# Turned tiles of a masked-softmax graph layer: half of them sent through DMA as f16 parts instead of through TensorE

## What is computed

```python
Wh = x @ W.T
sim = Wh @ Wh.T / (norms * norms.T + 1e-8)
alpha = softmax(where((adj > 0) | eye(N), sim, -inf), axis=1)
x1 = layernorm(x + alpha @ Wh)
mask = (adj > 0);  deg = sum(mask, axis=1)
agg = mask @ x1 / maximum(deg, 1.0)
comb = concat([x1 @ W_self + b_self, agg @ W_nb + b_nb]) @ W_comb + b_comb
out = layernorm(x1 + relu(comb))
```

## Time and profile before

| | us |
|---|---|
| Median of 3 runs | 889.4 (888.64 to 890.17) |
| The profiled execution | 888.87 |
| Its span | 887.1 |
| PE busy | 871.4 (98%) |
| DVE busy | 578.8 (65%) |
| ACT busy | 390.9 (44%) |
| POOL busy | 66.1 (7%) |

### The profile page before, as it was taken

One profiled execution on the slowest core, in us unless ns is written; L12 is line 12 of the kernel. 1 busy time (PEld: TensorE's weight loads), 2 busy tenths in 40 slices (PEclk: granted clock), 3 DMA queues, 4 the chain that ended last, 5 costly groups with the idle time before them and its releaser, 6 DMA issues.

```text
span 887.1 us, 20117 instructions
## 1 busy us (share of the span) xinstructions
PE 871.4 (98%) x7039; PEld 705.1 (79%) x7039; DVE 578.8 (65%) x1252; ACT 390.9 (44%) x661; POOL 66.1 (7%) x177
## 2 busy tenths in 40 slices
PE   8989999999999999999999999999999999999997
PEld 7767777777777777777787777777888888888886
DVE  3777877878666787668767877889716333333333
ACT  4867656655656565556565656564310000000000
POOL 3400000000000000000000000011101000000000
PEclk9999999999999999999999999999999999999999
DMA  8977675555554745576549459575753303311300
GB/s 223 292 175 184 186 209 154 158 170 154 149 169 131 215 139 168 151 178 189 163 141 240 136 171 316 157 202 114 203 113 126 113 19 113 114 66 67 114 18 19
DMA packets 165204, 135.72 MB, mean 153 GB/s; under 512 B 79121, under 2 KB 142882, under 8 KB 164098
## 3 DMA queue, kind: packets, MB, share of 16 engines
q1 hardware_dynamic: 164930, 134.26, 53.3%
q0 software_dynamic: 192, 0.41, 0.2%
HBM read 95.83 MB, written 28.85 MB: 141 GB/s over the span
## 4 chain that ended last, share of the span: by engine, by line
issue 81%; PE 9%; POOL 5%; DVE 2%; ACT 1%; POOLq 1%; DMA 0%; DVEq 0%; SPq 0%; ACTq 0%
PE ps L1142 3%; POOL rstd L571 3%; POOL var_eps L569 1%; PE ps L1230 1%; PE ps L1232 1%; PE ps L1231 1%; PE ps L1170 1%; PE ps L1172 1%; PE ps L1171 1%; PE ps L1224 1%; ACT mask L639 0%; DMA feat<-xT 0%; ACT prob_hi L634 0%; DVE feat L747 0%; DVE work L890 0%
## 5 line engine op out<-in xcount | busy, mean ns | idle before, releaser
L1230 PE MATMUL ps<-feat,prob_hi 128*128 128x257 f16 (+1 forms) x1024 | 279.8, 273 | 1.1 <-DVE prob_lo L897 1.1
L1232 PE MATMUL ps<-feat,prob_lo 128*128 128x257 f16 (+1 forms) x1024 | 279.5, 273 | 0.0
L1231 PE MATMUL ps<-feat,prob_hi 128*128 128x256 f16 (+1 forms) x1024 | 278.9, 272 | 0.0
L897 DVE SCALAR_TENSOR_TENSOR prob_lo<-work,prob_hi 128x512 f16<-128x512 f32 x256 | 176.0, 687 | 83.4 <-ACT prob_hi L634 80.7
L1373 PE MATMUL ps<-big,mgroup 128*128 128x257 f16 x992 | 219.2, 273 | 0.0
L1374 PE MATMUL ps<-big,mgroup 128*128 128x256 f16 x992 | 219.2, 273 | 0.0
L634 ACT ACTIVATE prob_hi<-work 128x512 f16<-128x512 f32 x256 | 154.4, 625 | 86.4 <-DVE work L890 42.8
L627 ACT ACTIVATE work<-ps 128x512 f32<-128x512 f32 (+2 forms) x144 | 79.2, 556 | 134.8 <-PE ps L1172 116.6
L639 ACT ACTIVATE mask<-work 128x1024 fp8e4<-128x1024 f32 x128 | 133.6, 1043 | 0.0
L1231 PEld LDWEIGHTS ps<-feat,prob_hi 128*128 128x128 f16 x1024 | 100.3, 98 | 25.3
L1230 PEld LDWEIGHTS ps<-feat,prob_hi 128*128 128x128 f16 x1024 | 100.0, 98 | 25.1 <-issue 1.3
(11 more groups left out here) (130 smaller groups left out, 780.9 us busy)
## 6 DMA issues: line engine op xcount, KB each, us to landing
adj_sb<-adjT SPq DMA_DIRECT2D x128, 512.0 KB, 3.8
mask_spill<-mask SPq DMA_DIRECT2D x128, 128.0 KB, 2.7
mgroup<-mask_spill SPq DMA_DIRECT2D x8, 2048.0 KB, 8.0
xres<-x SPq DMA_DIRECT2D x8, 512.0 KB, 5.1
x1h_dram<-big SPq DMA_DIRECT2D x16, 256.0 KB, 5.2
out<-rows SPq DMA_DIRECT2D x32, 128.0 KB, 1.7
feat<-xT SPq DMA_DIRECT2D x7, 512.0 KB, 6.7
unit_dram<-feat SPq DMA_DIRECT2D x7, 512.0 KB, 4.4
```

Of the source, the lines that this page charges most:

```text
L897: dve.scalar_tensor_tensor(out=prob_lo[:, s, :], in0=prob[:, s, :], scalar=PROB_SCALE, in1=prob_hi[:, s, :], op0=ALU.mult, op1=ALU.subtrac ...
L1230: pe.matmul(acc(D + 1), prob_hi[:, s, cols], feat_hi_of(g)[:, r, 0:D + 1], start=start, stop=False)
L1231: pe.matmul(acc(D), prob_hi[:, s, cols], feat_lo_of(g)[:, r, :], start=False, stop=False)
L1232: return pe.matmul(acc(D + 1), prob_lo[:, s, cols], feat_hi_of(g)[:, r, 0:D + 1], start=False, stop=stop)
```

## The change

In rows 1 to 6 (`far(a)`) a pair's eight tiles come in another order and two of its turned tiles by another way:

- Direct tiles 0 and 1: ScalarE writes the high f16 part of the unmasked exponential to `far_parts` (`high`), VectorE the low one (`low`). Both are then masked by f16 products: `keep` turns two tiles of int32 adjacency into an f16 0/1 mask (`kept`, in the place of a `prob` slot pair), and `masked_parts` multiplies it by both parts straight into `prob_hi` and `prob_lo`. ScalarE copies `kept` to `mask` (`unit_kept`).
- Direct tiles 2 and 3: as before.
- Tiles 4 and 5, the turned ones of `expo` 2 and 3: four transposes by TensorE each (`block_scores`), masked from PSUM (`mask_blocks`). A tile is now one block of 128 targets against four source blocks, added up within one tile (`attend_block`) and copied by one sum (`block_copied`).
- Tiles 6 and 7, the turned ones of `expo` 0 and 1: SP stores `far_parts` (512 KB) to `far_dram` and brings each part back by a transposing DMA (256 KB each) into `far_turned`; a second `keep` and `masked_parts` mask them. TensorE does nothing for them ahead of the attend.

SP's order in a pair: `store_far` of the next pair stands ahead of the fourth adjacency load, `turn_far` behind the last mask store; both wait. The loops of rows 1 to 6 are written out on every engine. `far_parts` lies in the place of `rows`, half of `far_turned` in that of `w0T_sb`; `damp` is halved. Semaphore counts follow.

```diff
+        def far_turned(h):
+            if h:
+                return far_turned_lo[:, :, :]
+            return w0T_sb[:, :, :].bitcast(F16).rearrange("p k n -> p (k n)").rearrange("p (s i) -> p s i", s=GB)
+        def kept(slot):
+            return prob[:, slot, :].bitcast(F16)
+        def halved(ap):
+            return ap.rearrange("p (s i) -> p s i", s=GB)
...
+            def load_next(a, b, m, slot):
+                if not far(a):
+                    load_unit(a, b, m, slot)
+                elif m < 2:
+                    load_direct(a, b, m, slot)
+                else:
+                    load_turned(a, b, 3 - m, slot)
...
+            def store_far(a, b):
+                k = far_before(a) + b - a - 1
+                sync.wait_ge(far_lo_ready, 2 * (k + 1))
+                sync.dma_start(far_dram.rearrange("h r p i -> p h r i"), far_parts).then_inc(far_stored, 16)
+            def turn_far(a, b):
+                k = far_before(a) + b - a - 1
+                if k == 0:
+                    sync.wait_ge(mixw_ready, 2)
+                sync.wait_ge(far_stored, 16 * (k + 1))
+                sync.wait_ge(prob_lo_ready, tiles_before(a)[0] + GB + (b - a - 1) * STEP_TILES)
+                for h in range(2):
+                    sync.dma_start_transpose(far_turned(h), far_dram[h].rearrange("r p i -> (r p) i")).then_inc(far_loaded, 16)
+            def pair_far(a, b):
+                t0 = tiles_before(a)[0] + GB + (b - a - 1) * STEP_TILES
+                u0 = tiles_before(a)[2] + 2 + (b - a - 1) * 4
+                for m in range(4):
+                    slot = (u0 + m) % 4
+                    if m == 3 and b < G - 1:
+                        store_far(a, b + 1)
+                    sync.wait_ge(prob_ready, t0 + 2 * m + 2)
+                    if b < G - 1:
+                        load_next(a, b + 1, m, slot)
+                    elif m < 2:
+                        load_direct(a + 1, a + 1, m, slot)
+                    elif a + 2 < G:
+                        load_next(a + 1, a + 2, m - 2, slot)
+                    sync.wait_ge(mask_ready, u0 + m + 1)
+                    if m < 2:
+                        store_direct(a, b, m, slot)
+                    else:
+                        store_turned(a, b, 3 - m, slot)
+                if b < G - 1:
+                    turn_far(a, b + 1)
...
+            def unit_kept(u, s, count):
+                act.wait_ge(kept_ready, count)
+                wait(act, mask_stored[u % 4], 16 * (u // 4))
+                act.activation(mask[:, u % 4, :], kept(s), ACT.Copy, saturate=False).then_inc(mask_ready, 1)
...
+            def pair_far(a, b):
+                n = b - a - 1
+                t0, f0, u0 = (first + more for first, more in zip(tiles_before(a), (GB + n * STEP_TILES, GB + n * GB, 2 + n * 4)))
+                c0 = scores_before(a) + GB + n * 6
+                k = far_before(a) + n
+                if n == 0:
+                    act.wait_ge(mirror_done, (a + 1) * (GB - 1))
+                def high(r):
+                    act.wait_ge(exp_ready, f0 + r + 1)
+                    if k == 0:
+                        act.wait_ge(mixw_ready, 2)
+                    wait(act, far_stored, 16 * k)
+                    act.activation(far_parts[:, 0, r, :], expo[:, r, :], ACT.Copy, scale=PROB_SCALE).then_inc(far_hi_ready, 1)
+                for r in range(2):
+                    exponentials(t0 + r, c0 + r, f0 + r, r, GB)
+                    high(r)
+                unit_kept(u0, 0, 2 * k + 1)
+                for r in range(2, GB):
+                    exponentials(t0 + r, c0 + r, f0 + r, r, GB)
+                    heads(t0 + r, r)
+                unit_mask((u0 + 1) % 4, 2, 16 * ((u0 + 1) // 4))
+                heads(t0 + 4, 0)
+                heads(t0 + 5, 1)
+                unit_blocks(u0 + 2, 0)
+                unit_kept(u0 + 3, 2, 2 * k + 2)
...
+            def block_copied(b, block, t):
+                dve.wait_ge(attn_done, t + 1)
+                to = partial_of(b)[:, block, :]
+                dve.tensor_tensor(to, to, turned_ps(block % 2, D + 1), ALU.add).then_inc(turned_copied, 1)
+            def keep(u, s, parts):
+                dve.wait_ge(prob_lo_ready, parts)
+                dve.wait_ge(adj_loaded[u % 4], 16 * (u // 4 + 1))
+                wait(dve, mask_ready, u - 1)
+                dve.tensor_scalar(kept(s), adj_sb[:, u % 4, :], 0.0, None, ALU.is_gt).then_inc(kept_ready, 1)
+            def masked_parts(t, s, adj, high, low, shaped):
+                wait(dve, attn_done, t - GB + 1)
+                dve.tensor_tensor(shaped(prob_hi[:, s, :]), adj, high, ALU.mult).then_inc(prob_ready, 1)
+                dve.tensor_tensor(shaped(prob_lo[:, s, :]), adj, low, ALU.mult).then_inc(prob_lo_ready, 1)
+            def pair_far(a, b, between):
+                n = b - a - 1
+                t0, f0, u0 = (first + more for first, more in zip(tiles_before(a), (GB + n * STEP_TILES, GB + n * GB, 2 + n * 4)))
+                c0 = scores_before(a) + GB + n * 6
+                h0 = heads_before(a) + GB + n * GB
+                k = far_before(a) + n
+                loaded = lambda m: 16 * ((u0 + m) // 4 + 1)
+                def low(r):
+                    dve.wait_ge(far_hi_ready, 2 * k + r + 1)
+                    dve.scalar_tensor_tensor(out=far_parts[:, 1, r, :], in0=expo[:, r, :], scalar=PROB_SCALE, in1=far_parts[:, 0, r, :],
+                                             op0=ALU.mult, op1=ALU.subtract).then_inc(far_lo_ready, 1)
+                def beside(count=1):
+                    for _ in range(count if between else 0):
+                        if between:
+                            between.pop(0)()
+                more = 2 if a == G - 2 else 1
+                for r in range(2):
+                    damping(a, b * GB + r, c0 + r, f0 + r, r)
+                low(0)
+                low(1)
+                keep(u0, 0, t0)
+                dve.wait_ge(kept_ready, 2 * k + 1)
+                dve.wait_ge(far_lo_ready, 2 * k + 2)
+                for r in range(2):
+                    masked_parts(t0 + r, r, kept(0)[:, r * GW:(r + 1) * GW], far_parts[:, 0, r, :], far_parts[:, 1, r, :], lambda ap: ap)
+                beside(more)
+                damping(a, b * GB + 2, c0 + 2, f0 + 2, 2)
+                dve.wait_ge(prob_lo_ready, t0)
+                mask_direct(h0, f0 + 2, 2, 2, u0 + 1, (u0 + 1) % 4, loaded(1))
+                beside(more)
+                damping(a, b * GB + 3, c0 + 3, f0 + 3, 3)
+                mask_direct(h0, f0 + 3, 3, 3, u0 + 1, (u0 + 1) % 4, loaded(1))
+                tails(t0 + 2, 2, h0)
+                beside(more)
+                if n:
+                    block_copied(b - 1, 0, t0 - 2)
+                    block_copied(b - 1, 1, t0 - 1)
+                dve.wait_ge(prob_lo_ready, t0 + 2)
+                mask_blocks(c0 + 4, 0, 0, u0 + 2, loaded(2))
+                tails(t0 + 3, 3, h0 + 1)
+                beside(more)
+                mask_blocks(c0 + 5, 1, 1, u0 + 2, loaded(2))
+                keep(u0 + 3, 2, t0 + 3)
+                tails(t0 + 4, 0, h0 + 2)
+                beside(more)
+                tails(t0 + 5, 1, h0 + 3)
+                beside(2 * more)
+                dve.wait_ge(kept_ready, 2 * k + 2)
+                dve.wait_ge(far_loaded, 32 * (k + 1))
+                for x in range(2):
+                    cols = slice(x * P, (x + 1) * P)
+                    masked_parts(t0 + 6 + x, 2 + x, halved(kept(2))[:, :, cols], far_turned(0)[:, :, cols], far_turned(1)[:, :, cols], halved)
+                    block_copied(b, 2 + x, t0 + 4 + x)
...
+            def block_scores(r, f):
+                pe.wait_ge(exp_ready, f + 1)
+                for x in range(GB):
+                    ins = pe.transpose(score_ps(r)[:, x * P:(x + 1) * P], expo[:, r, x * P:(x + 1) * P], ident[:, :])
+                ins.then_inc(score_done, 1)
+            def attend_block(a, t, s, x, copied):
+                pe.wait_ge(prob_lo_ready, t + 1)
+                pe.wait_ge(turned_copied, copied)
+                for r in range(GB):
+                    ins = add_up(lambda w: turned_ps(x, w), s, slice(r * P, (r + 1) * P), a, r, r == 0, r == GB - 1)
+                ins.then_inc(attn_done, 1)
+            def front_far(a, b, j):
+                n = b - a - 1
+                t0, f0 = tiles_before(a)[0] + GB + n * STEP_TILES, tiles_before(a)[1] + GB + n * GB
+                if j < 2:
+                    direct_scores(a, b * GB + j, t0 + j, j, 0, (prob_ready, t0 + j - (3 if n else 1)))
+                elif j < GB:
+                    direct_scores(a, b * GB + j, t0 + j, j, 0, (exp_ready, f0 + j - 1))
+                elif j < GB + 2:
+                    block_scores(j - 2, f0 + j - 2)
+            def pair_far(a, b):
+                n = b - a - 1
+                t0 = tiles_before(a)[0] + GB + n * STEP_TILES
+                copied = GB * (pairs_before(a) + n) - 1
+                for j in range(STEP_TILES):
```

(70 more changed lines are left out.)

90 lines of the change are left out of this document (59 added, 31 removed).

## The result

The changed kernel takes 880.45 us in the median (878.5 to 880.51, 4 runs), the kernel before beside it 889.63 (888.64 to 890.17, 4 runs): a ratio of 0.989, 95% interval 0.988 to 0.991, 9.2 us faster. The profiled execution takes 880.43 us, its span is 878.6. The forecast was 877.

The account below looks back on a forecast made before the run. TensorE's matmul pitch was taken to bound rows 1 to 6. From 888.9 us: -18.1 + 3.5 + 1.5 + 3.6 = -9.5, with old stops -12.5 at best, so -12: 877 us, range 870 to 891.

Parts of the forecast that it names:

- Removed: TensorE, rows 1 to 6: 42 turned tiles at 0.43 us no longer pass through it, 18.1 us less.
- VectorE's new work: VectorE in a pair: 11.3 us plus 3.3 of pieces, covered by 16.6; f16 products taken at 0.42 us each.
- Pieces: Normalisation operations of the previous row on VectorE, ahead of tail 3: 0.35 us late in ten pairs, 3.5 us.
- Row 6: Row 6's only pair: 14 normalisation pieces run, six of them ahead of tail 3, costing 1.5 us.
- Turn of a row: First pair of each row, where VectorE and ScalarE have no lead: 0.6 us a row, 3.6 us in all.
- Old stops: TensorE's existing stops in rows 1 to 6, 3 us, mostly go with the hand-offs that replace them.
- DMA: Turned parts by store and transposes: chain 9.9 to 13.3 us, queue 79% full, costed at nothing in steady pairs.
- The rival's break point: Rival of late transposes ahead of tile 6: decides when the chain exceeds 14.6 us; 906 us, chance 0.13.
- Written-out rows: Loops of rows 1 to 6 written out: taken as nothing, with 1 us either way.

Follow-up runs that it names:

- the doubled turns: The changed kernel with each remaining turn by TensorE issued twice into the same place: 893.28 us, a pair 17.49 us.
- the last experiment: The changed kernel with xres loaded early in rows 1 to 5, row's sums before last products, keep first in first pairs, pieces behind tail 3 in rows 1 to 4: 872.88 us.

## Why the prediction was nearly right, step by step

- **Removed:** 18.1 us forecast and 18.1 measured, by pairs of 17.47 and 16.61 us and, from the other side, by the doubled turns. The turns by TensorE outside the diagonals, L1483 and L1449, are 280, as named.
- **VectorE's new work:** products 0.42 us as taken. They were the largest unknown, and the forecast's sign depended on them: at 0.69 the kernel is 8 us slower than before.
- **Pieces:** 3.5 us forecast for ten pairs, 2.2 measured in five: 0.2 in each second pair of rows 1 to 4, where I had 0.35, and 1.4 in row 5's last pair, ahead of tiles 3 and 4 (0.57 and 0.80 us). The other five, first pairs, stop for exponentials 2 and 3. Row 6: 1.5 forecast, 3.8 measured. Its only pair carries all pieces and stops ahead of the turn of exponential 3 (1.55 us), of tile 3 (0.56) and of tile 4 (1.59), where I had followed the chain to tail 3 only.
- **Turn of a row, the step that failed:** "I take 0.6 us a row, 0 to 1.5: 6 x 0.6 = 3.6". Measured 6.3, still inside the bounds of that sentence but 2.7 off its value. I followed the chain of exponentials, far tails and products to tile 0. The first pairs do stop, 1.9 us in all, but at the turns of exponentials 2 and 3 and not at tile 0, and 1.4 of the 1.9 went when the diagonal ahead of them was on time: that this part looks well priced is luck. I left out that diagonal, and in it VectorE's wait for the `xres` load. It was in the rows (L931, 6.5 us of idle), nearly hidden before. The diagonals of rows 2, 3, 4 and 6 lost 0.60 to 0.82 us by it, 3.0 in all. The earlier load took away the 2.2 of rows 2 to 4, and with the 1.4 of the first pairs and row 6's loss of 0.8 its 3.3 us come about; row 6's own stop went in the last experiment. The remaining 1.4 of the 6.3 are 0.2 in each of five diagonals, which the row's sums in their new place remove, and 0.4 in row 1's.
- **Old stops:** 2.5 to 3 us to vanish; 3.7 of the 5.4 did.
- **DMA:** share 79% estimated, 81% measured; no transpose late for TensorE. The rival's break point, a chain of 14.6 us, came from TensorE's demand for tile 6. The loop through VectorE closes earlier, at 16.6 less 3.3, or 13.3 us. It decided nothing at 8.8, itself below my 9.9 to 13.3, but at the upper end of my own range, 13.3, the room would have been none.
- **Written-out rows:** nothing forecast, nothing measured.

Sum: -18.1, new stops 12.3 where 8.6 were forecast (row turns +2.7, row 6 +2.3, pieces -1.3), old stops -3.7, small steps +0.5: -9.0 against -12. The mechanism, turns taken from TensorE against new hand-offs at row turns and beside pieces, was right. The terms at the row turns and in row 6 were too small, the first because the residual's load was missing from the chain.

## What to carry to other kernels

When work is taken from the engine that sets the end, list all idle rows of the other engines at the places with little lead, the hidden ones too: a load for which VectorE waited up to 1.4 us, nearly all of it beside TensorE's work, became a stop of 0.6 to 0.8 when the change came, and issuing it earlier was worth 3.3 us after the change and nothing that can be told before it. For a chain through DMA with one set of buffers, measure the whole loop until the next store, not only the time to the consumer. And a reordering that clears one hand-off has to be read on SyncE's queue too, for it moves every transfer behind it.

## What the runs showed of the chip that was not expected

- A two-operand f16 product of 512 elements lasts 418 to 422 ns, the same by the three-operand form 683 to 688. A one-source compare of 1024 int32 elements into f16 lasts 686 ns, as long as 512 of the two-source mask; I had taken 755.
- With the DMA share in quiet stretches from 0.53 to 0.81, plain transfers landed later, by the medians of the whole span: mask stores of 128 KB after 4.9 us instead of 2.7, adjacency loads after 5.2 instead of 3.8. A 512 KB store to `far_dram` took 3.4 in the median, but 7.6 and 8.5 where it was issued 6.5 to 7 us behind the 2 MB load.
- The issue of a 256 KB transpose of the far parts held SyncE for 1.23 and 1.31 us in the median (1.61 at most), less than the 2.1 that the earlier trace rows gave as the median.
